# A recommendation tower with table lookups by matmul: four groups of fields in every quarter, paced gathers, and a new order of all work

## The reference

```python
e = stack([tbl_f[ids[:, f]] for f in range(40)], axis=1)      # (2048, 40, 32)
z[b, k] = einsum('bke,kef,bkf->bk', e[:, I], W, e[:, J])       # 780 pairs i < j
h = concatenate([z, dense_ctx], axis=1)                        # 780 + 16
h = maximum(h @ W_top1 + b_top1, 0)                            # 512
h = maximum(h @ W_top2 + b_top2, 0)                            # 256
y = h @ W_top3                                                 # 1
```

## Time and profile before

| | |
|---|---|
| runs | 632.9, 632.92, 633.13 us |
| span of the profiled execution | 1130.1 us (no other time of this execution is given) |
| TensorE busy | 875.4 us, 7232 matmul instructions |
| VectorE busy | 540.3 us, 510 |
| ScalarE busy | 327.1 us, 243 |
| GpSimd busy | 412.3 us, 436 |
| gathers issued | 432 |

### The profile page before, as it was taken

How to read it: one execution, slowest core, us unless ns; L and a number is a source line. 1 busy time by engine, 2 the same in 40 slices (tenths; PEclk the granted TensorE clock), 3 DMA queues, 4 the chain that set the end, 5 groups by cost and what they waited for, 6 DMA issues and landing times.

```text
span 1130.1 us, 16792 instructions
## 1 busy us (share of the span) xinstructions
PE 875.4 (77%) x7232; PEld 201.8 (18%) x7232; DVE 540.3 (48%) x510; ACT 327.1 (29%) x243; POOL 412.3 (36%) x436
## 2 busy tenths in 40 slices
PE   4322358788779995886895789779889787899998
PEld 1000012121112220121121112112112111122223
DVE  3100067364345660452380447337245264688884
ACT  4001047553246380032260134127244000000002
POOL 6777341533353137324517151451624604000000
PEclk8555598887578895886796788989779788899999
DMA  4100044201001020100101002010010102011010
GB/s 155 32 14 13 12 145 127 63 7 52 9 11 53 12 72 13 44 16 18 38 22 41 5 10 75 9 47 4 12 34 8 39 3 58 8 39 29 1 36 3
DMA packets 30489, 39.24 MB, mean 35 GB/s; under 512 B 11376, under 2 KB 19200, under 8 KB 30160
## 3 DMA queue, kind: packets, MB, share of 16 engines
q1 hardware_dynamic: 14880, 25.59, 7.7%
q0 software_dynamic: 13824, 7.11, 4.3%
q10 hardware_dynamic: 1712, 5.48, 1.4%
HBM read 21.93 MB, written 0.07 MB: 19 GB/s over the span
## 4 chain that ended last, share of the span: by engine, by line
PE 65%; another core or an unknown queue 17%; issue 11%; DVE 3%; ACT 2%; SPq 1%; DMA 1%; DVEq 0%; ACTq 0%
PE t_ps L857 27%; PE z_ps L881 18%; PE x_ps L898 10%; PE x_ps L806 7%; PE x_ps L911 2%; SPq L543 1%; DVE prod L727 1%; ACT one_hot L602 1%; PE t_ps L911 1%; DVE one_hot L689 1%; PE t_ps L898 1%; PE t_ps L829 0%; DVE z_sb L673 0%; ACT one_hot L605 0%
## 5 line engine op out<-in xcount | busy, mean ns | idle before, releaser
L727 DVE TENSOR_TENSOR prod<-t_ps,e_t 128x1024 f32<-128x1024 f32 x392 | 459.4, 1213 | 425.2 <-remote 300.6
L558 POOL DMA_INDIRECT rows<-cold_tables,idx x432 | 412.1, 954 | 550.1 <-DVE e_t L734 420.2
L857 PE MATMUL t_ps<-e_t,w_sb 32*64 32x512 f32 x3120 | 362.0, 658 | 73.8 <-issue 53.6
L881 PE MATMUL z_ps<-prod,select 128*32 128x512 f32 x1560 | 243.5, 639 | 21.7 <-issue 21.0
L602 ACT ACTIVATE one_hot<-hot_sb,row_number 128x2048 bf16<-128x2048 f16 (+1 forms) x75 | 140.6, 1875 | 110.3 <-remote 87.4
L898 PE MATMUL x_ps<-z_sb,w_sb 128*32 128x512 f32 x704 | 131.1, 635 | 24.4 <-issue 22.5
L605 ACT ACTIVATE one_hot<-one_hot 128x2048 bf16<-128x2048 bf16 (+1 forms) x75 | 134.3, 1791 | 2.4
L857 PEld LDWEIGHTS t_ps<-e_t,w_sb 32*64 32x64 f32 x3120 | 74.6, 136 | 323.0 <-issue 221.6
L806 PE MATMUL x_ps<-one_hot,tables 128*32 128x512 bf16 x1194 | 97.8, 402 | 27.3 <-issue 22.6
L806 PE MATMUL t_ps<-one_hot,tables 128*32 128x512 bf16 x198 | 45.3, 501 | 92.1 <-issue 87.9
L689 DVE TENSOR_SCALAR one_hot<-hot_sb,row_number 128x2048 bf16<-128x2048 f16 (+1 forms) x47 | 33.9, 744 | 133.2 <-remote 130.0
(11 more groups left out here) (33 smaller groups left out, 98.6 us busy)
## 6 DMA issues: line engine op xcount, KB each, us to landing
e_t<-e_t SPq DMA_DIRECT2D x64, 128.0 KB
e_t<-e_t SPq DMA_DIRECT2D x112, 64.0 KB
rows<-cold_tables,idx POOLq DMA_INDIRECT x432
hot_sb<-hot_ids SPq DMA_DIRECT2D x11, 512.0 KB, 3.6
w_sb<-w_lay ACTq DMA_DIRECT2D x1, 1792.0 KB, 7.0
z_sb<-hot_tables SPq DMA_DIRECT2D x4, 320.0 KB, 5.1
w_sb<-w_lay ACTq DMA_DIRECT2D x1, 1216.0 KB
w_sb<-w_lay ACTq DMA_DIRECT2D x1, 896.0 KB, 4.6
```

Of the source, the lines that this page charges most:

```text
L558: pool.indirect_dma_start(out=rows[:, slot, span, :], out_offset=None, in_=table, in_offset=bass.IndirectOffsetOnAxis(ap=idx[:, n, span:sp ...
L727: nc.vector.tensor_tensor(prod[:, u % PROD_SLOTS, 0:banks, :], t_ps[:, at:at + banks, :], by, ALU.mult).then_inc(mult_done, 1)
L857: mm = nc.tensor.matmul(t_ps[cols, at + n, :], w_sb[part, b, cols], e_t[part, e_slot(k, of[side]), :], start=True, stop=True)
L881: mm = nc.tensor.matmul(z_ps[E * q:E * q + E, :], select[:, E - PER - PER * s:2 * E - PER - PER * s], prod[:, (u + q // 2) % PROD_SLOTS, q ...
```

## The change

`HOT` becomes `[4,4,4,4]`: 16 items are looked up, 24 gathered. `ORDER` is written anew. GpSimd gets a pace: the table `PACE` gives for each gathered item n a first and a last place in the order, the item's 16 gathers are spread evenly over these in twos, and before each two GpSimd waits until the last `g` before that place has had its products made, or the last `h` before it (one that doesn't end its item) has been done, whichever of the two is nearer.

Steps by letter, for the whole order and for its part up to the 28th `g`:

| | g | r | h | o | O | t | p | 1 | 2 | 3 | all |
|---|---|---|---|---|---|---|---|---|---|---|---|
| before | 200 | 196 | 122 | 47 | 75 | 27 | 32 | 96 | 32 | 8 | 837 |
| after | 200 | 196 | 152 | 73 | 79 | 24 | 32 | 96 | 32 | 8 | 894 |
| before, to the 28th g | 28 | 25 | 57 | 36 | 24 | 4 | 32 | 0 | 0 | 0 | 208 |
| after, to the 28th g | 28 | 25 | 63 | 40 | 26 | 4 | 32 | 0 | 0 | 0 | 220 |

(Two steps `i`, which spread the first ids, are in all four rows. Of the 32 steps `p`, VectorE and ScalarE do 16 each.) The turns `t` of the new order stand at places 112, 146, 162, 177, 221, 262, 335, 342, 359, 362, 441, 478, 490, 519, 521, 524, 583, 600, 715, 733, 760, 771, 792 and 835.

```diff
--- before.py
+++ after.py
@@ -23,7 +23,7 @@
 
 HOT_GROUPS = 4
 
-HOT = [4,3,3,3]
+HOT = [4,4,4,4]
 TABLE_PARTS = 3
 HOT_SLOTS = 4
 
@@ -162,14 +162,15 @@
 
 
 ORDER = """
-pippppipphpoohoOppoohopphpohOppohpoophphpopohhhooOhpoohpohhopohphhpotopOhhohhhpgpoophhhphOhrhoohhoooppghhhOooh
-oOgorhhhOgOhhgOrghrogrrgrOgrthgOhrgOhhgrOhgrgrorgrhghOOrtgrhOgrghOhOOgOrhgrghrOtgrrghrghhgrghOroOgrrghOhgrrtgr
-hgrghhgOOrhgOrgrgOtOrrghOrghOhgrgrgrgohrgrrOgrghhOgrhOghrgrohgrOhgOhrg1trOgO1rg1rtOgr1g11grrg1trgr1g11g1r1grhg
-OrohhgOhrhogtrOhghOhrgrrghrOghrOOgt1111gr1g1rgrrgOhhhoOgrorghhhgrOhgrrOoghrhhg1tO1grrgt11g1rgr1Ogrrg2rgr2g2rg2
-Org2trgO22gr2grhgrOhgrOhgrOhghorgrhhghrgrt1g1rg11gro11grrg1t1g1OrrgO1Org11grrghhgrhOOgrhogOrrhghrOghrOgthrghrh
-Og1rgt11gr1Og1Or1gr3g3OrgOrhgrhogrhOhgrhOghrgrhgrhgrhtrOgrOhg11g11tgr11grr2g2rgrrgr2g2rg2rg22gr2g3rgrgr3grtrg1
-1grgrg1t1gr1grgr1grrg11grrgt11g1rgr1grrg1rg11gt1rgr1gr1grrg1rgrg1trg11g1rg1rgrrg2rg22tg2rgr2g2rgr2g2rgr1g1rgr1
-g1rgr1gtr1g1rgrrg1rg11gr1g1rgrrg11gr1gr1grrg33g1r1r1111112222222233
+pppppippoopOppopoiopphphoooohphppOpohhooohhpopphhOhhhpOohhpoohhphohphpoohhOhpophogoOhhhpopohghOoohhrpprohgOhoh
+hotooghhohOhrhgrOghhgrghroOgOrohrOgrthghrOgrgrghhgrhtOghrOorgOrhhohtOOghhgOrhOoOgrrgOohhgrrghhgrOorghrOghhgrOg
+rtrgOrhghohOgrhgorOhOgrrghhgoOhrgrhgrrogOhtrOhOghhgrorOgrhghhgrhgOrorgrhgOhrghrgOrhg1O1gO11grorg11grrg11g1rgro
+rg111tOrghohthogohrrhhgOhorhgthhtrOg1or1grO11g11grrgOohhhoghOrohhoghOhrgohOrhgorrghrgOOhhghorgOOrrghrghhgrhgrh
+gtrrgOrOhg1rg1O1rgr1g11grrg2Org22g2rgOtrrgr2g2rg2rt2OghhgOorrghrOghrgOrhghhghrgt1t1rtg1OO1rgr11rgo11g1rg1O11gr
+hhgrhgOhrorgOhrghhOgrorghrgrOhgrhtg1Or1oo1Og111gr3t3rhghhOgOrohhogOrorOhgrhghhgoOhrOgrrghrhoghOhgorhghrOrghhgr
+orgrOhhg1rg11g1rg11grr2gr2grrgr2gr2g2rgr2g22g3rgrrgr3g1t1g1rgrgrg1rg11grrtgr1g1rg11grrg11grrgr1gr1g1trg11gr1gr
+rtgr1g11gr1g1rgr1grrgrt2g22gr2grg2rgrrg2gr2g2rgrrgr1gr1g11grgr1grt1gr1g1rgr1g1rg1rgr1grrg1rg1rg11gr3gr3g11rr11
+11112222222233
 """
 
 START = [(0, 0), (1, 0), (0, 1), (0, 2), (1, 1), (0, 3), (1, 2), (2, 0), (1, 3), (2, 1), (2, 2), (3, 0), (2, 3), (3, 1),
@@ -217,6 +218,19 @@
             assert read < min(n for n, step in enumerate(steps) if step[:2] == (below, k + 1) and use_of(step)[2])
     assert at["o"] == len(lookups) and all(at[letter] == len(kind) for letter, kind in kinds.items())
     return steps
+
+
+PACE = [
+    0, 77, 107, 137, 167, 211, 252, 280, 304, 328, 352, 394, 418, 442, 466, 490, 514, 566, 590, 686,
+    710, 734, 758, 782, 825,
+]
+TOGETHER = 2
+
+
+def pace_of(n, span):
+
+    begin, end = PACE[n], PACE[n + 1]
+    return begin + (end - begin) * (span - span % TOGETHER) // SPANS
 
 
 def use_of(step):
@@ -486,6 +500,16 @@
             a, b = (begin_of(c) for c in W_PIECES[n])
             engine.dma_start(w_sb[:, a:b, :], w_lay[:, a:b, :]).then_inc(w_loaded[n], 16)
 
+        def wait_for_pace(engine, place):
+
+            for kind, *of in reversed(steps[:place]):
+                if kind == "gen":
+                    engine.wait_ge(mult_done, first_unit(*of) + 2)
+                    return
+                if kind == "hot" and of[2] < blocks[of[1]] - 1:
+                    engine.wait_ge(looked_up, looked_up_to[tuple(of)])
+                    return
+
         @block.sync
         def _(sp):
             sp.dma_start(row_number[:, :], row_numbers).then_inc(numbers_loaded, 16)
@@ -555,6 +579,8 @@
                 if n >= ROW_SLOTS:
                     pool.wait_ge(turned, n - ROW_SLOTS + 1)
                 for span in range(SPANS):
+                    if span % TOGETHER == 0:
+                        wait_for_pace(pool, pace_of(n, span))
                     pool.indirect_dma_start(
                         out=rows[:, slot, span, :], out_offset=None, in_=table,
                         in_offset=bass.IndirectOffsetOnAxis(ap=idx[:, n, span:span + 1], axis=0),
```

## The result

The changed kernel takes 667.43 us (665.48 to 668.04), the kernel before 633.02 us (632.9 to 633.54): a ratio of 1.0527, 95% interval 1.0501 to 1.0554. It is slower by 34.4 us, where 21.5 were forecast (654.4 for 632.9).

A forecast was written before the change was run, and what follows sets the result against it. TensorE was taken to bound the kernel. To 632.9 us came 20.0 for added lookups and the first stage and 1.5 for late turns, fewer gathers counting 0: 654.4 us, range 638 to 668.

The forecast's parts named there:

- The bound before: Kernel before: TensorE's 591 us of work, idle only in the first stage, set a span floor of 617.5 us.
- the first stage: Order up to the 28th g, where VectorE's work sets the pace: ends at 116 us before, 119 after.
- the 15 us between floor and median: Kernel before: gap from the 617.5 us span floor to the 632.92 us median, put down to time outside the span and small waits.
- The gathers before: GpSimd's queue in the kernel before: 20.0 us an item, 16 us early at the end, close but not binding.
- Parts (1) to (3): Three more items looked up on TensorE (+21.2 us), their one-hots mostly hidden, and the first stage: together +20.0 us.
- Part (5): Three more loads of spread ids and three more copies on ScalarE with x_ps taken: between 0 and 3 us, taken as 0.
- Part (6): Pacing of GpSimd's gathers: late turns of 19 us at most, about 12 reaching the end, taken as 1.5 us.
- The other signs: Expected in the trace: 1752 bf16 matmuls, VectorE busy some 558 us, GpSimd some 366, and waits on products or lookups.
- Rival A: Late items: pacing at its upper end of 12 us plus 3 us of part (5), 668 us; chance 0.15.
- Rival B: Faster: gathers also slow TensorE without a profiler, so fewer of them win back up to 30 us, 623 us; chance 0.13.

The follow-up runs named there:

- experiment 9: Kernel before with each of GpSimd's 432 indirect DMAs replaced by a plain DMA of 128 neighbouring rows: 632.61 us, where the kernel before took 1144.54.
- experiment 10: Changed kernel with plain DMAs of neighbouring rows in place of the indirect ones: 646.58 us, ratio 1.0194 to the kernel before at 633.51 us.
- experiment 6: Changed kernel with 240 of the 360 added lookup matmuls left out: 820.84 us, against 823.11 us for the changed kernel on such a chip.
- Experiment 11: Changed kernel with plain DMAs cut into two or three pieces, to occupy GpSimd about as long as gathers, pace kept: 658.61 us.
- experiment 2: Changed kernel without the waits for the pace: 1116.0 us, against 1143.33 us for the kernel before on the same chip.
- experiments 3 and 8: Changed kernel with its pace 24 places earlier: 842.14 us, ratio 0.738; with items ending 16 places ahead and taking at least 30: 828.89 us, ratio 0.724 to kernel before.
- experiments 10 and 12: Changed kernel with undivided plain DMAs, paced: 646.58 us; with plain DMAs cut to about the gathers' length and no waits for the pace: 646.04 us.

## Why the prediction was right, and where it was off

The bound, the direction and the places of the late turns were right. The measured time lies inside the range by 0.6 us, 13 us above the forecast of 654.4, and two errors of opposite sign are in it: the work was priced 7 us too high, the late turns some 20 us too low.

**The bound before.** The sum said that TensorE is never idle behind the first stage, with the 28th g at 116 us and a span of 617.5. Experiment 9 has TensorE idle for 20 us in all, and its 28th g at 116.2. (As added, VectorE's 111.4 us from 3.8 on end at 115.2 and not 116, and the 114.4 at 118.2 and not 119; the difference stands.) The span is 630.6: the part behind the first stage takes 514 us, not 501. From the starts of all matmuls behind the 28th g of that run, a g takes 1.08 us and not 1.04, which makes 6.5 of the 13 us, and an h of 12 matmuls 0.77 and not the best case's 0.705, which with three more of them there makes 6; r, 1 and 2 are at 0.925, 0.93 and 0.91. The 15 us between floor and median, which I put down to "what lies outside the span and small waits", are thus mostly steps that are a little longer; about 2 us lie outside.

**The gathers before.** That they are close but do not bind is borne out by experiment 9, at 0.1%, on a chip of the other kind.

**Parts (1) to (3), +20.0 us.** It is +13.1 in time (646.58 for 633.51) and +13.9 between the spans of experiments 9 and 10. The first stage is as forecast, 119.1 for 116.2 us, against 119 for 116. What is off is TensorE behind it: 525 for 514 us, +11 instead of +17. By the starts of the matmuls there, the 24 added h make all h 14.9 us longer (62.6 for 47.7), 0.62 each and not 0.705, and all g became 2.2 us and layer 1 1.8 us shorter, though their number is the same. So each of the three gives a third of the missing 6 us. The step that was off is the one that took everything but the added h as unchanged by the new order: in both orders the steps hold small waits, and the new one has fewer (an h of 12 at 0.73 instead of 0.77). That was only reckoned from the traces and not tried by a run: a thinner lookup was run only where it decides nothing (experiment 6).

**Part (5), x_ps and the ids:** taken at 0. No cost of it shows in the 13.1 us, which are less than the lookups' own price; it wasn't measured by itself.

**Part (6), the pace.** This is the term that was mis-sized. The working gave late turns before items 9 and 15 of 3 and 9 us and "at most 7" at items 2 and 3, 19 us together. The trace of after has 5.3, 4.5 and 8.0 at items 3, 9 and 15, 17.8 us, and a rest of 0.3. So the lateness was right in its places and nearly in its sum. The working then let at most 12 us of it reach the end, and took 1.5 of them. Two things are wrong with that.

First, TensorE's own stops are 12.2 us in the trace: the bound of 12 was the right number for what the filled banks let through, and nothing lowered it further. The reason given for 1.5, that stalls make the places longer and so give the gathers time, fails because a paced queue starts the next item from a place too: when the order stands still, the pace's places stand still with it. From the start of item 11 to the end of item 15 GpSimd made no pause; the 80 gathers took 100.4 us, where the working had reckoned 100.

```profile
252.88 0.95 POOL L584 DMA_INDIRECT rows<-cold_tables,idx  x1 [0.30 <-issue]
...
352.33 0.95 POOL L584 DMA_INDIRECT rows<-cold_tables,idx  x1 [0.30 <-issue]
```

Second, the sum has no term for the clock. Some 20 us of the run pass at the low clock at and behind the three stops, and TensorE is busy 635.3 us for the same 7592 matmuls that take it 626.7 in experiment 10: 8.6 us. With the idle time, 30.6 us instead of 17.8, that makes the whole difference of the two spans, 665.9 - 644.5 = 21.4 us. In time it is 667.43 - 646.58 = 20.9 us, on two chips whose times for the kernel before differ by 0.5. Experiment 11 divides in the same way: 5.6 us more of idle time, 7.3 more of busy time.

The page's mark of this was in the earlier trace rows: TensorE has no idle time there, so the filled banks are all that lies between a stop of VectorE and one of TensorE, and after the stop both have work that neither can do faster.

**The other signs.** The trace has the 1752 bf16 matmuls, VectorE busy 553.3 us (558 forecast), GpSimd 373.0 (366), GpSimd waiting on products, and the waits before items 3, 9 and 15 that were named for rival A. The gathers beside VectorE's one-hots are as in the earlier trace rows: of the 384 gathers 21 took longer than 1.1 us, and all 21 overlap a one-hot; the 69 that overlap one take 1.08 us on average, the others 0.95. The mean of all is 971 ns for 954 before, 384 by 0.017 = 6.5 us of GpSimd's queue.
The Trainium skill's rule on the shared port (SBUF — State Buffer, "SBUF: two separate sides") agrees with that: a VectorE operation in a two-port mode keeps GpSimd from writing descriptors. By amount it is one third of what the late turns came to.

**Rival A** (0.15) is what happened in its mechanism, 668 us forecast and 667.43 measured, but not in its sum: late turns gave 21 us and not 12, the work 13 and not 20, and the 3 us of part (5) nothing that shows. That the total agrees is chance, and so is that the time falls just inside the range.

**Rival B** had the right effect and the wrong place. Gathers do hold up TensorE, by 500 us, on the chips where the profile was taken, and the pace is worth 0.755 there. On the chip of the comparison nothing of it was there to win: experiment 9 equals the kernel before.
By the Trainium skill (Runtime: NRT & Kernel Launch, "Instruction fetch mechanics") instructions are streamed in blocks of 16 KiB, at a cost mostly hidden. Late blocks do not show as what differs: the queue of instruction blocks moved 57 packets and 0.93 MB in experiment 9 as in the kernel before at 1130 us, at a mean of 1.17 and 1.15 us each, and none was moved between 62 and 149 us of the latter, where the lone matmuls of the earlier trace rows stand.

**What stays open.** What sets the two kinds of chip apart, whether it is the chip at all, and by what way an indirect DMA of GpSimd holds up TensorE's issue there. On a quick chip no version with real gathers was run beside the two kernels: that taking away the pace (experiment 2) or starting items earlier (experiments 3 and 8) removes the late turns there, for some 646 us by experiments 10 and 12, was not tried. The kernel before is the fastest one measured on a quick chip, and without late turns the new order is still 13 us behind.

## What to carry to other kernels

Where one engine has no idle time, a wait elsewhere costs what is left of it when it reaches that engine, and the work at the lower clock behind it on top (12.2 and 8.6 us here); discount no late transfer for slack that the profile doesn't show on the engine that binds. A pace for a queue must be made from the queue's own time per item (20 us here), not from a count of places (24, some 17 us); the test is to make the transfers shorter or to take the pace away, and with plain DMAs in the gathers' place each alone removed the late turns.

Before anything is explained, hold the profiled execution's length against the timed one. Here 1130 us beside 633 meant two different sets of conditions, in one of which the change costs 34 us and in the other saves 309.

## What the runs showed of the hardware

On four of the five chips of these experiments, indirect DMAs issued by GpSimd without a pause held TensorE's matmuls down, in the worst stretches to one in 2.8 us at a granted clock of 0.50, and the kernel before took 1132 to 1145 us; on the fifth it took 633.51 us with the same code. Replacing them by plain DMAs of neighbouring rows, of the same size and from the same queue, gave 632.61 us on one of the four. Waits that are already satisfied between them changed nothing (1145.83 us); waits that pause them for progress of the order gave 821 to 853 us. An indirect DMA occupied GpSimd for 1.25 us, start to start, on both kinds of chip, and a plain one of 128 rows for 0.53 us; indirect ones that overlapped a one-hot of VectorE lasted 1.08 us on average and the others 0.95. Around the ends of stops of TensorE of 3.86, 2.32 and 5.99 us the granted clock was 0.50 for 6.8, 3.4 and 10.2 us.
